# Where a twelve-layer decoder splits its contexts: two engines, another place in the step

## The reference, cut to what matters

```python
q = (x @ Wq).reshape(B, T, 2 * H, D).transpose(0, 2, 1, 3) * scaling      # 16 heads of 32
k, v = jnp.split(x @ Wkv, 2, axis=-1)                                     # 8 value heads of 64
attn_w = softmax(einsum('bhqd,bhkd->bhqk', q, k))
attn_w = attn_w.reshape(B, H, 2, T, T)
attn_w = attn_w[:, :, 0] - lam * attn_w[:, :, 1]
attn = einsum('bhqk,bhkd->bhqd', attn_w, v)
rms = sqrt(mean(attn * attn, axis=-1))
attn = gamma * (attn / (rms + EPS)) * (1.0 - LAMBDA_INIT)
x = layernorm(x + attn.reshape(B, T, 512) @ Wout)
...
x = layernorm(x + cross_attention(x, ctx_768))      # second layer: the first that needs the context
```

## Time and profile before

| what | value |
|---|---|
| median of 3 runs | 1853.83 us (1852.09 to 1861.79) |
| profiled execution, its time | 1857.34 us |
| its span, 41105 instructions | 1855.5 us |
| mean granted TensorE clock | 0.938 |
| busy: TensorE | 1606.8 us, 87% |
| busy: VectorE, ScalarE, GpSimd | 942.2, 707.4, 423.4 us |
| first layer's steps | from about 13 to 188 us |

### The profile page before, as it was taken

One profiled execution on the slowest core, in us unless ns is written; L12 is line 12 of the kernel. 1 busy time (PEld: TensorE's weight loads), 2 busy tenths in 40 slices (PEclk: granted clock), 3 DMA queues, 4 the chain that ended last, 5 costly groups with the idle time before them and its releaser, 6 DMA issues.

```text
span 1855.5 us, 41105 instructions
## 1 busy us (share of the span) xinstructions
PE 1606.8 (87%) x14780; PEld 1320.9 (71%) x14780; DVE 942.2 (51%) x2542; ACT 707.4 (38%) x1646; POOL 423.4 (23%) x667
## 2 busy tenths in 40 slices
PE   6888899889994879998799488995897999899998
PEld 5766677668992757776689366773685777689897
DVE  2454677731104556777311472445444667575765
ACT  2222677512231326654122124550464656311110
POOL 2121676720005331111100433431121111000101
PEclk9887999999996999998899799996898999999999
DMA  4333200068871002110586201101001000023232
GB/s 180 111 101 145 83 27 25 21 223 303 309 283 46 2 1 78 29 27 11 220 303 237 68 1 43 39 26 45 1 1 58 28 26 13 24 81 102 84 121 66
DMA packets 41849, 166.69 MB, mean 90 GB/s; under 512 B 5984, under 2 KB 16864, under 8 KB 30176
## 3 DMA queue, kind: packets, MB, share of 16 engines
q1 hardware_dynamic: 39392, 159.14, 24.6%
q0 software_dynamic: 2304, 5.51, 1.0%
HBM read 140.21 MB, written 24.41 MB: 89 GB/s over the span
## 4 chain that ended last, share of the span: by engine, by line
PE 65%; DVE 11%; issue 10%; POOL 6%; ACT 3%; DMA 3%; DVEq 0%; SPq 0%; POOLq 0%; ACTq 0%
PE bank L1616 6%; PE bank L1629 6%; PE bank L1241 6%; PE bank L1228 4%; PE bank L1566 4%; PE bank L1568 4%; PE bank L1567 4%; PE bank L1255 2%; PE bank L793 2%; PE bank L784 2%; PE bank L1211 2%; PE bank L1216 2%; PE bank L885 1%; PE bank L1203 1%; PE bank L830 1%
## 5 line engine op out<-in xcount | busy, mean ns | idle before, releaser
L1990 ACT ACTIVATE arena<-big,nm 112x375 f32<-112x375 f32 x384 | 215.8, 605 | 30.4 <-DVE nm L2737 16.8
L1241 PEld LDWEIGHTS bank<-cst,arena 112*125 112x125 f32 x1152 | 148.0, 194 | 54.9 <-issue 30.1
L1241 PE MATMUL bank<-cst,arena 112*125 112x112 f32 x1152 | 169.5, 285 | 8.6 <-ACT big L2000 4.8
L3020 POOL TENSOR_TENSOR mv<-mv,cst 112x1 f32<-112x1 f32 x104 | 23.8, 229 | 627.4 <-DVE mv L2192 627.0
L2115 ACT ACTIVATE htile<-bank,wup 128x128 f32<-128x128 f32 x280 | 79.9, 369 | 182.8 <-PE bank L1616 182.8
L1616 PE MATMUL bank<-xtile,wup 128*128 128x128 f32 x1120 | 132.1, 277 | 0.3 <-DVE xtile L2830 0.3
L1616 PEld LDWEIGHTS bank<-xtile,wup 128*128 128x128 f32 x1120 | 129.3, 194 | 0.6 <-DVE xtile L2830 0.5
L1629 PE MATMUL bank<-wdn,htile 128*128 128x256 f32 x560 | 126.3, 379 | 0.0
L2845 DVE COPY yrow<-bank 128x256 f32<-128x256 f32 x35 | 14.9, 425 | 217.3 <-PE bank L1629 217.3
L1780 ACT COPY xT<-bank 128x224 f32<-128x224 f32 (+1 forms) x96 | 33.3, 347 | 239.3 <-PE bank L765 233.6
L765 PE MATMUL bank<-cst,xln 112*128 112x112 f32 x176 | 39.9, 313 | 94.8 <-DVE xln L2198 77.5
(11 more groups left out here) (351 smaller groups left out, 3605.8 us busy)
## 6 DMA issues: line engine op xcount, KB each, us to landing
wup<-in_moe_up SPq DMA_DIRECT2D x35, 1028.0 KB, 7.2
wdn<-in_moe_dn SPq DMA_DIRECT2D x35, 1024.0 KB, 6.0
vspace<-in_ring SPq DMA_DIRECT2D x40, 512.0 KB, 4.0
ctxs<-parts SPq DMA_DIRECT2D x30, 564.0 KB
slots<-mlpw SPq DMA_DIRECT2D x11, 1024.0 KB, 6.5
parts<-ctxs SPq DMA_DIRECT2D x8, 564.0 KB, 3.1
xrow<-slots SPq DMA_DIRECT2D x35, 128.0 KB, 4.8
slots<-yrow SPq DMA_DIRECT2D x35, 128.0 KB, 6.7
```

The costliest lines, as they stand in the source:

```text
L1241: mm = pe.transpose(bank[4 + (3 * g + t) % 2][0:KT, j * T:(j + 1) * T], c_pr[:, g, j, t * KT:(t + 1) * KT], ident[0:T, 0:T])
L1990: nc.scalar.activation(c_pr[:, g, j, :], c_sc[:, g % 2, j, :], ACT.Exp, bias=nm[:, p, h:h + 1], scale=-1.0).then_inc(cexp_done, 1)
```

## The change

In `step` of `diff`, ScalarE calls `split_context` (and `split_kv` in step 7) right after the copy of the queries and ahead of the exponentials, and no longer at the end of the step. VectorE calls them ahead of `values_in` and no longer behind it. Operations, operands and waits are the same.

```diff
@@ ScalarE, diff, step
                     if more:
                         queries(b + 1, 1 - p)
                     if back[0]:
+                        split_context(b, p)
+                    if isinstance(b, int) and b == B - 1:
+                        split_kv(SUBS[sub.index + 1])
+                    if back[0]:
                         exps(b)
                     if one:
                         output_columns_d(b - 1)
...
                     if more:
                         value_rows(b + 1, 1 - p)
-                    if back[0]:
-                        split_context(b, p)
-                    if isinstance(b, int) and b == B - 1:
-                        split_kv(SUBS[sub.index + 1])
@@ VectorE, diff, step
                         rows_out(sub, b - 2, p)
                     if back[0]:
-                        values_in(b)
-                    if back[0]:
                         split_context(b, p)
                     if isinstance(b, int) and b == B - 1:
                         split_kv(SUBS[sub.index + 1])
+                    if back[0]:
+                        values_in(b)
```

## The result

The changed kernel takes 1828.33 us (median of 4 runs, 1825.9 to 1829.5) against 1857.81 us for the kernel before in all its runs so far (4, 1852.1 to 1863.2). The ratio is 0.984 with a 95% interval of 0.980 to 0.988, so 23 to 37 us of gain. Forecast were 1823 us and 31 us less. The profiled execution took 1825.9 us with a span of 1824.0, which is 31.5 us less than the span before.

A forecast was written before the change was run, and what follows sets the result against it. The first layer's stage was taken as bound by one turn of in-order queues, 2.47 us from scores to maxima. Order 20.1 + clock 11 = 31 us, so 1853.8 - 31 = 1823 us; eight in ten from 1812 to 1838.

The forecast's parts named there:

- What bounds the stage: First layer's stage: in-order queues, with VectorE's subtraction waiting 2.23 us for ScalarE's rounding, put 2.47 us between scores and maxima.
- VectorE, what goes: VectorE's turn without the subtractions: maxima 2.45 us earlier, 2.25 in the first turn; with last turn and drain 20.1 us.
- The clock: TensorE in the first layer's stage: shorter gaps keep full clock, worth 9.5 us over six turns; 11 us taken in all.
- the turn at full clock: One batch element's scores to the next's with TensorE at full clock: 15.3 us, summed from rows, six making 91.8.
- Step 7 and the drain: Last turn and drain of the stage: order gives 2.3 and 3.3 us, held clock another 2.5 (between 0 and 4).
- What comes, on ScalarE and VectorE: Moved rounding ahead of the exponentials (1.6 us room) and moved subtractions (1.14 us) under VectorE's 5.07 us idle: cost nothing.
- GpSimd: GpSimd's copy and residual addition beside VectorE's moved subtractions: may wait up to 1.14 us a step, the sum stays.
- The sum: Whole kernel: 31 us less, 1823 us against the 1853.8 median; nothing after the stage takes the gain back.
- The signs: Profile marks: maxima within 0.1 us of scores, TensorE idle under 0.6, clock full to about 140, scores 15.3 us apart.
- order without clock: Rival: maxima come 2.45 us earlier but TensorE's clock still falls in every step; 20 us gain, 1834 us; chance 18%.
- a new wait: Rival: VectorE's subtractions or the squares become the chain; gain 22 us (1832), or 11 us (1843) without clock; chance 11%.
- slower: Rival: ScalarE's rounding, now ahead of the exponentials, waits for SyncE's write or load; 1868 us; chance 2%.

The follow-up runs named there:

- e1: Changed kernel with only ScalarE's move kept, VectorE's subtractions standing as in the kernel before; 1833.7 us, ratio to before 0.986.
- e2: Kernel before with only VectorE's subtractions moved, each taking the context of the step before; 1829.4 us, ratio to before 0.985.
- e3: Kernel before with two 512-column warming matmuls behind the queries in steps 1 to 6; 1850.1 us, ratio to before 0.995.
- e8: Changed kernel with two 256-column warming matmuls in step 7 and two of 512 columns in the first draining step; 1824.7 us, ratio to before 0.979.
- e9: e8 with two more 256-column warming matmuls behind the queries of step 1; 1824.8 us, ratio to before 0.980.
- e7: Changed kernel with three more ScalarE roundings per step ahead of each context's rounding; 1828.7 us, ratio to before 0.982.
- e6: Changed kernel with six more VectorE subtractions per step, written to unused memory; 1827.7 us, ratio to before 0.981.
- e5: Changed kernel with two more VectorE subtractions per step, written to unused memory; 1828.3 us, ratio to before 0.982.
- e4: Changed kernel with two 256-column warming matmuls in step 7 ahead of the products with the values; 1826.2 us, ratio to before 0.982.

## Why the prediction was right, step by step

*What bounds the stage.* Right. The wait of VectorE's queue was the turn's bound; e1 shows that it was the wait and not the work, and e2 that removing it from VectorE's side alone does the same.

*VectorE, what goes.* 2.45 us a turn were predicted; e3 against the changed kernel gives 2.43. In the first turn the maxima wait for the squares, as said: they start 0.83 us behind the scores' end (36.23 against 35.40), and 2.33 us go where 2.25 were predicted.

*The clock.* Predicted were 9.5 us for six turns. e3 shows 2.00 us for each of the five turns from 2 on, so 10 without the first, and that TensorE's gap, not its narrow matmuls, is the cause. Six turns took 116.7 us before and 90.0 after, 26.7 less where the sum had 24.0; with 14.5 us of order in it the clock's share is 12.2. The term mis-sized is the turn at full clock, 15.3 us against 14.89: from the end of the scores to the products it had 6.80+0.60 = 7.40 us and measured are 102.56-95.58 = 6.98, since in step 0 the products had been held by the exponentials and the added transposition falls in part into that wait. The rest of the turn was 7.90 us as taken.

*Step 7 and the drain.* Predicted 2.3+3.3+2.5 = 8.1 us, measured 34.5-27.1 = 7.4. The assumption that the clock would hold there was wrong: it fell at about 134 us behind a gap of 1.38 us before the products, and these took 4.92 us, longer than the 3.85 before. The slow projection then held the residual, and the sum of squares began 0.6 us after the squares' end and not with it. With full clock through both places this part takes 25.0 us (e8, e9), so the fall costs 2.1. That the gap of 1.38 us alone brings it about is not shown: in e1 and e7 the clock held behind the same gap.

*What comes, on ScalarE and VectorE.* Cost nothing, as said. Room ahead of the exponentials 1.57 us (predicted 1.6), idle time ahead of the first reciprocal 1.14 us after. The prediction thought the subtractions' cover to be that idle time; e6 shows that it goes 1.65 us beyond.

*GpSimd.* Its copy went from 0.40 to 0.46 us and its addition from 0.64 to 0.94, beside subtractions of which the second went from 0.55 to 0.65. The price was in the predicted bounds and on no path. The Trainium skill (SBUF — State Buffer, "Who interferes with whom") says that two such instructions shut each other out; e6, where the copy lasts 3.22 us beside the six added subtractions (2.85 us) and the first of its own, agrees. In the changed kernel, e5 and e6 alike the copy ends 0.24 to 0.25 us after the start of the last subtraction.

*The sum.* 31 us predicted, 29.5 measured between the medians, 31.5 between the profiled spans. The stage gave 34.1, more than forecast; 3.6 us of that are missing from the span because the later layers took 1671.5 us and not 1667.9. In the ten other profiles the same code took 1670.9 to 1678.1 us, 1672.3 in e3, whose order is that of before. So I take the profile of before for a short one and not the 3.6 us for a cost of the change; with one profile of that kernel this is not shown. Why it varies was not tried. That the forecast 31 comes so near to 31.5 is in part luck: the turns gave 2.7 us more than the sum had, the last step and the drain 0.7 less, the forecast had rounded the clock's 12 us down to 11, the first scores came 1.0 us early, and the later layers took 3.6 back.

*The signs.* The maxima begin 0.02 us after the scores' end, TensorE idles 0.32 us ahead of their transposition, and no exponential waits for a rounding, as said. Three signs came out otherwise: the clock is full to about 134 us and not to 140, the scores are 14.89 us apart and not 15.3, and in step 0 the subtraction does wait for ScalarE, 0.31 us, without delaying the reciprocals, which come as long after the products as before.

The rival "order without clock" fell with the windows of the changed kernel, "a new wait" with e5 to e7, "slower" with the rounding that starts right behind the copy of the queries (98.02 us; the copy is recorded as ending at 97.59+0.53 = 98.12) and waits for no transfer.

## What to carry to other kernels

Look at what stands, in an engine's written order, ahead of the reader of the critical operand. Here the instruction that waited for another engine cost its wait of 2.23 us, and its length (1.14 us) only the 0.15 us that the engine had no slack for, and moving either the waiting one or the one awaited was enough. Put side work where its engine waits for the bound engine anyway, and count the idle times behind that place as cover too. A gap in TensorE's work can cost twice, once as time (here 2.43 us a turn) and once as the clock of what follows (2.00), so the second part has to be in the sum.

## What was not expected

The clock's fall behind a short gap is not settled by the program. In the first turn, with a gap of 1.2 us ahead of L863 and the same instructions, one profile (e8) shows 0.50 from 42 to 44 us and a turn of 17.15 us, seven others a turn of 15.57:

```profile
42.00:44.00 2.00, 2.00 (x52) 2.00 (x51) 1.46 (x3) 0.00 (x0) 0.00 (x0) 0.50 0.00 0
```

The same holds for step 7, where the clock fell in five of seven profiles with the same gap of 1.38 us. One profile of such a place proves little. And where the clock held in step 7, warmed (e4) or not (e1, e7), it fell behind the next gap, 10 to 13 us later, unless that was filled too (e8, e9), so that about 0.5 us (e4, e7) were left of the 3 expected; e1, whose drain is longer by its subtractions, gained nothing.
